# A long convolution per channel: four chunks joined by modal states in place of Toeplitz cross products

## What is computed

```
K = 2.0 * jnp.einsum('hn,hnl->hl', Cs, jnp.exp(P)).real    # P = dtA * l, 64 modes n per channel h, 1024 steps l
y = jnp.fft.irfft(u_f * k_f, n=n)[..., :Lq]                # causal convolution of each row with its channel's K
y = y + u_m * D[:, None]
x = x + y * mask                                           # the mask cuts each batch at its length
x = x + lora_8(x, adapter of the batch)                    # rank 16, 8 adapters
x = x + lora_64(x, adapter of the batch)                   # rank 16, 64 adapters
x = x + W[subject].T @ x + bias[subject]                   # 64x64 per batch
```

## Time and profile before

| | us |
|---|---|
| median of 3 runs (lowest, highest) | 754.1 (753.35, 757.32) |
| the profiled execution's own time | 756.05 |
| its span, first to last instruction | 754.2 |
| PE, DVE, ACT, POOL busy | 715.3, 576.9, 434.5, 380.6 |
| setup stage, in the span | 0 to 35.9 |
| turn 0 | 35.9 to 92.6 |
| turns 1 to 4 | 92.6 to 315.5 |
| turns 5, 6, 7 | from 315.5, 368.3 and 419.5; the last product ends at 468.5 |
| pair stage, from its first transposes | 479.0 to 754.2 |

### The profile page before, as it was taken

How to read it: one execution, slowest core, us unless ns; L and a number is a source line. 1 busy time by engine, 2 the same in 40 slices (tenths; PEclk the granted TensorE clock), 3 DMA queues, 4 the chain that set the end, 5 groups by cost and what they waited for, 6 DMA issues and landing times. The chain is left out here.

```text
span 754.2 us, 19782 instructions
## 1 busy us (share of the span) xinstructions
PE 715.3 (95%) x6685; PEld 538.6 (71%) x6685; DVE 576.9 (76%) x1116; ACT 434.5 (58%) x760; POOL 380.6 (50%) x680
## 2 busy tenths in 40 slices
PE   2699999999999999999899999699999999999997
PEld 2377687787787787777677777477767777776774
DVE  7687987887886776876667665288888888888885
ACT  4535645645635636636335332277777777777775
POOL 1000088888885000047777200667676676767663
PEclk9799999999999999999999999899999999999999
DMA  6488989999899899899888982789999999999973
GB/s 209 119 277 246 325 281 335 282 362 332 293 368 359 273 356 337 292 311 296 288 249 269 321 291 118 297 272 315 315 311 323 315 324 316 319 320 319 317 259 154
DMA packets 121719, 219.97 MB, mean 292 GB/s; under 512 B 20226, under 2 KB 80194, under 8 KB 121666
## 3 DMA queue, kind: packets, MB, share of 16 engines
q1 hardware_dynamic: 102546, 166.56, 68.2%
q10 hardware_dynamic: 9904, 33.59, 11.6%
q0 software_dynamic: 9216, 19.15, 7.9%
HBM read 146.35 MB, written 72.91 MB: 291 GB/s over the span
## 5 line engine op out<-in xcount | busy, mean ns | idle before, releaser
L1078 PE MATMUL ps<-toep,xTh 128*128 128x512 f16 (+3 forms) x1024 | 210.3, 301 | 4.3 <-DMA diff<-d_rows 3.4
L1078 PE MATMUL ps<-toep,xTl 128*128 128x512 f16 (+3 forms) x512 | 147.4, 301 | 0.0
L1078 PEld LDWEIGHTS ps<-toep,xTh 128*128 128x128 f16 x1024 | 97.5, 98 | 56.5 <-DMA diff<-d_rows 4.3
L825 POOL DMA_INDIRECT gnow<-g_rows,idx_g x64 | 59.6, 931 | 115.9 <-DMA g_rows<-g_out 89.6
L801 POOL DMA_INDIRECT wnow<-in_L_cond_weights,idx_w x64 | 62.6, 978 | 100.7 <-DVEq L1015 83.6
L1271 POOL DMA_INDIRECT asel<-a_rows,idx_a x64 | 72.0, 1125 | 77.5 <-PE ps L1417 76.4
L1044 DVE TENSOR_TENSOR ps<-ps,common 128x512 f32<-128x512 f32 x64 | 44.6, 697 | 66.3 <-ACT common L867 66.0
L1266 POOL COPY bsel<-bt 128x256 f16 x256 | 92.7, 405 | 2.8 <-issue 2.2
L1356 DVE TENSOR_TENSOR xTl<-ps,xTh 128x1024 f16<-128x1024 f32 x64 | 78.4, 1224 | 13.6 <-ACT xTh L1315 10.3
L1078 PE MATMUL ps<-diff,xTh 128*128 128x256 f16 x512 | 87.3, 273 | 0.0
L217 DVE TENSOR_TENSOR xTl<-ps,xTh 128x1024 f16<-128x1024 f32 x64 | 77.7, 1214 | 0.0
(11 more groups left out here) (231 smaller groups left out, 1719.2 us busy)
## 6 DMA issues: line engine op xcount, KB each, us to landing
toep<-k_rows SPq DMA_DIRECT2D x64, 384.0 KB, 6.1
diff<-d_rows SPq DMA_DIRECT2D x64, 384.0 KB, 7.3
xt<-in_x SPq DMA_DIRECT2D x32, 512.0 KB, 6.4
x_rows<-xt ACTq DMA_DIRECT2D x32, 512.0 KB, 4.9
xt<-x_rows SPq DMA_DIRECT2D x32, 512.0 KB
out_dram<-outt SPq DMA_DIRECT2D x32, 512.0 KB, 7.9
out_dram<-diff SPq DMA_DIRECT2D x32, 512.0 KB
toep<-x_rows SPq DMA_DIRECT2D x24, 512.0 KB, 7.4
```

The costliest lines, as they stand in the source:

```text
L825: gp.indirect_dma_start(m.gnow[:, v, :], None, m.g_rows, bass.IndirectOffsetOnAxis(ap=m.idx_g[0:64, q:q + 1], axis=0)).then_inc(g_gathered ...
L1078: last = PE.matmul(out, xs[x_part], rhs(part), start=start and k == 0, stop=stop and k == 2)
```

## The change

The convolution of a channel is cut into four chunks of 256 samples. Within a chunk it stays a Toeplitz product (`within`, with a matrix of 256 columns only). What earlier chunks do to a later one goes through the 128 modal states: `state` forms the state at the end of a chunk from its two blocks of x (table U, `ut`) and, for the second and third, from the state before (table R, `rt`, two numbers per mode spread over a matrix); `from_state` adds the state's effect to the next chunk (table V, `vt`). Each state leaves PE, is split by ACT (`high_state`) and DVE (`low_state`), and goes back to PE. One bank of PSUM holds the high half of the output, where there were two. The fourth chunk's last product (`finish_high`) runs behind the next channel's transposes.

The tables U, V and R are made per 8 channels by ACT, DVE and POOL, and POOL's own run of 32 units is cut up between its table work. The Toeplitz tables shrink from 768 to 128 KB a channel.

The diff, cut to its core:

```diff
+def high_state(nc, m, act, h, u, n):
+
+    act.wait_ge(m.s_done, 3 * h + n + 1)
+    nc.scalar.activation(m.sh[:, u % 2, n, :], state_bank(m, u, n), ACT.Copy, scale=1 / S_SCALE).then_inc(m.s_high, 1)
...
+def low_state(nc, m, dve, h, u, n):
+
+    dve.wait_ge(m.s_high, 3 * h + n + 1)
+    nc.vector.scalar_tensor_tensor(m.sl[:, u % 2, n, :], state_bank(m, u, n), 1 / S_SCALE, m.sh[:, u % 2, n, :],
+                                   ALU.mult, ALU.subtract).then_inc(m.s_ready, 1)
...
+def wide_products(nc, m, gp, k, e):
+
...
+    for n, part in enumerate((m.uc, m.us)):
+        nc.gpsimd.tensor_tensor(m.pu[:, :, :, n, :], part[:, :, cut, :], m.ue[:, :, cut, :], ALU.mult).then_inc(m.pu_ready, 1)
...
+def v_second(nc, m, gp, k, e):
...
+    nc.gpsimd.tensor_tensor(m.v2[:].rearrange("p q (a b) -> p q a b", b=TB),
+                            *by_steps(m, m.a2[:, KP * e:KP * e + KP, :], m.es, e), ALU.mult).then_inc(m.v2_ready, 1)
...
+def v_join(nc, m, dve, k, e):
+
+    dve.wait_ge(m.v1_ready, 2 * k + e + 1)
+    dve.wait_ge(m.v2_ready, 2 * k + e + 1)
+    nc.vector.tensor_tensor(m.v1[:], m.v1[:], m.v2[:], ALU.subtract).then_inc(m.v_made, 1)
...
+def turn_matrices(nc, m, gp, k, e):
+
...
+    for n, part in enumerate((m.rch, m.rcl)):
+        nc.gpsimd.tensor_tensor(m.rt[:, cut, n, :].rearrange("p q (s n) -> p q s n", s=2),
+                                m.eyeh[:].unsqueeze(1).unsqueeze(1).broadcast_to([P, KP, 2, N]),
+                                part[:, cut, :].unsqueeze(3).broadcast_to([P, KP, 2, N]), ALU.mult).then_inc(m.r_ready, 1)
...
-                def all_pairs(gather, keep, read):
-                    for q in range(U):
-                        gather(q)
-                    for k in range(PAIR_TURNS):
-                        if k < PAIR_TURNS - 1:
...
-                            for q in range(U * (k + 1), U * (k + 2)):
-                                gather(q)
-                        keep(k)
...
+                for i in range(TURNS):
+                    if i:
+                        turn_matrices(nc, m, gp, i, 1)
+                    else:
+                        turn_matrices(nc, m, gp, 0, 1)
+                    v_second(nc, m, gp, i, 1)
+                    if i == 1:
...
+                    if 1 <= i <= 5:
+                        w_unit(3 * i - 3)
+                    if i < TURNS - 1:
+                        wide_products(nc, m, gp, i + 1, 0)
+                        turn_columns(nc, m, gp, i + 1)
+                        turn_matrices(nc, m, gp, i + 1, 0)
+                        if 1 <= i <= 5:
+                            w_unit(3 * i - 2)
+                        if i == 6:
+                            for k in range(0, 5):
+                                g_unit(k)
+                        v_second(nc, m, gp, i + 1, 0)
+                        wide_products(nc, m, gp, i + 1, 1)
+                        if 1 <= i <= 5:
+                            w_unit(3 * i - 1)
+                        if i == 5:
+                            w_unit(15)
+
+                            gp.wait_ge(m.g_stored, 16 * G)
+                            for q in range(U):
+                                gather_g(q)
+                for k in range(5, PAIR_TURNS):
+                    g_unit(k)
...
+                        high_state(nc, m, act, h, u, 0)
+                        if not (last and u == XU - 1):
...
+                        high_state(nc, m, act, h, u, 1)
...
+                        if u == 2:
+                            if first:
...
+                        if make_k and u == 3:
+                            narrow_pairs(nc, m, act, i + 1)
+                            wide_cos(nc, m, act, i + 1)
...
+                        high_state(nc, m, act, h, u, 2)
...
+                        if make_k and u == 0:
+                            narrow_exp(nc, m, act, i + 1)
+                            wide_exp(nc, m, act, i + 1)
+                        if make_k and u == 1:
+                            narrow_trig(nc, m, act, i + 1)
+                        if make_k and u == 2:
+                            wide_sin(nc, m, act, i + 1)
+                            wide_abs(nc, m, i + 1)
+                        if make_k and u == 4:
+                            high_u(nc, m, act, i + 1, 0)
+                        if start_k and u == 6:
+                            act.wait_ge(m.pu_ready, 4 * i + 8)
+                            load_modes(m, act, i + 2)
+                        if make_k and u == 7:
+                            high_u(nc, m, act, i + 1, 1)
...
+                        if group and u % U == 1:
+
+                            act.wait_ge(a_loaded, 16 * g)
+                            S.activation(by_k.rearrange("p (k a r) -> p k a r", k=J, a=8),
+                                         nat_a.rearrange("p (a k r) -> p k a r", a=8, k=J), ACT.Copy).then_inc(a_ordered, 1)
...
+                        low_state(nc, m, dve, h, u, 0)
+                        if u == 0:
+                            low_u(nc, m, dve, i, 1)
+                        if u == 1:
+                            v_join(nc, m, dve, i, 1)
+                        if make_k and u == 3:
+                            narrow_mix(nc, m, dve, i + 1)
+                        if make_k and u == 4:
+                            k_first(nc, m, dve, i + 1, 3)
+                        if make_k and u == 5:
+                            low_u(nc, m, dve, i + 1, 0)
+                        if start_k and u == 7:
+                            narrow_turns(nc, m, dve, i + 2)
+                        if not (first and u == 0):
+
+                            dve.wait_ge(conv_done, h)
+                            select(h - 1, u - 1, 1, x1_ready)
+                        low_state(nc, m, dve, h, u, 1)
                         if not (last and u == XU - 1):
                             low_x(nc, m, dve, h + 1, u + 1)
...
+                        select(h, u, 0, low_ready)
+                        low_state(nc, m, dve, h, u, 2)
+                        if u == 0:
+                            v_first(nc, m, dve, i, 1)
                         if make_k and u == 1:
-                            k_tables(nc, m, dve, i + 1)
-                        if make_k and u == 3:
-                            k_first(nc, m, dve, i + 1, 3)
+                            wide_fraction(nc, m, dve, i + 1)
+                        if make_k and u == 2:
+                            narrow_modes(nc, m, dve, i + 1)
+                        if u == 2:
+                            low_v(nc, m, dve, i, 1)
                         if make_k and u == 4:
+                            v_first(nc, m, dve, i + 1, 0)
                             k_low(nc, m, dve, i + 1, 3)
...
+                        if make_k and u == 5:
+                            v_join(nc, m, dve, i + 1, 0)
+                        if make_k and u == 6:
+                            low_v(nc, m, dve, i + 1, 0)
+                        if group and u % U == 1:
...
+                    out = state_bank(m, u, n)
+                    if n == 0:
+                        pe.wait_ge(m.xTl_ready, h + 1)
+                        if v % KP == 0:
+                            pe.wait_ge(m.u_ready, 2 * i + 1 + u // KP)
+                    for b in range(2):
+                        for k, (x_part, part) in enumerate(((m.xTh, 0), (m.xTl, 0), (m.xTh, 1))):
+                            last = PE.matmul(out, m.ut[:, b, v, part, :], x_part[:, u % 2, 2 * n + b, :],
+                                             start=(b == 0 and k == 0), stop=(n == 0 and b == 1 and k == 2))
+                    if n:
+                        pe.wait_ge(m.s_ready, 3 * h + n)
+                        if n == 1 and v % KP == 0:
+                            pe.wait_ge(m.r_ready, 2 * (2 * i + v // KP + 1))
+                        for k, (part, before) in enumerate(((0, m.sh), (0, m.sl), (1, m.sh))):
+                            last = PE.matmul(out, m.rt[:, v, part, :], before[:, u % 2, n - 1, :], start=False, stop=(k == 2))
+                    last.then_inc(m.s_done, 1)
...
+                def from_state(i, u, c):
...
+                    pe.wait_ge(m.s_ready, 3 * h + c)
+                    if c == 1 and u % KP == 0:
+                        pe.wait_ge(m.v_ready, 2 * i + u // KP + 1)
...
                         if not (last and u == XU - 1):
                             turn(i, u + 1)
-                        convolve(i, u, first and u < 2)
-                        g = 2 * i - 1 + u // U
+                        if not (first and u == 0):
+                            if u:
+                                finish_high(i, u - 1)
...
+                        pe.wait_ge(m.toep_loaded[u % U], 16 * (2 * i + 1 + u // U))
+                        if not (first and u == 0):
+
+                            pe.wait_ge(low_ready, h)
+                        within(u, 0)
+                        state(i, u, 1)
+                        within(u, 1)
```

(10 more changed lines are left out.)

671 lines of the change are left out of this document (375 added, 296 removed).

## The result

The changed kernel took **886.2 us** (median of 4, 885.7 to 887.8) beside 755.7 us for the kernel before on the same chip: ratio 1.173, 95% interval 1.167 to 1.178. Slower was forecast, and the place of the largest single stall; but 886 is 60 us above the forecast and 30 above the end of its range.

A forecast was written before the change was run, and what follows sets the result against it. PE was taken as the bound, spending columns. Setup +5, turns 1 to 4 +29, turn 6 +27 and the tail +11, together +72 on 756.05, gave 828 us, 826 for the median; 8-in-10 range 775 to 856.

The forecast's parts named there:

- Turn 6 and POOL's 64 us: PE stands 24.5 us in turn 6 behind five adapter units (+27 for the turn); POOL works 64 us in turn 7.
- Rival (d): DVE's join of V does not wait for POOL's gathers, if POOL had passed them early enough; no chance of its own.
- A plain channel of PE: A channel's products and transposes take PE 5.22 us, against 6.10 before; -56 us over 64 channels if nothing waits.
- rival (b): Local waits vanish wholly and PE stays the bound: 748 us; chance 0.13.
- Turns 1 to 4: Four group turns at 48.1 us of PE, 14 of waits and 1 more: 252 against 222.9, +29 us.
- The walk through the queues: PE's waits for ACT, DVE and POOL, read from their queues: about 5 us a plain turn, below 14 a group turn.
- rival (c): DVE and POOL block each other at SBUF: 5 us a turn passed on, POOL delayed 2, +25: 852 us; chance 0.17.
- four in ten: Of some 19 added DVE operations a turn, four in ten meet POOL and lose 0.6 us: 5 us a turn.
- Turn 5 and turn 0: Turn 5 takes 53 us against 52.8 and turn 0 57 against 56.7: 0 for both.
- Setup: The first tables' longer chain of steps on ACT, DVE and POOL lengthens setup by 5 us, bounds 3 to 8.
- The tail: Turn 7 to the pair stage: POOL 64 us, barrier 2, filler matmuls 4.5, so 70.5 against 59.5: +11.
- rival (a): POOL's waits come, local ones mostly don't: 2 us a plain and 6 a group turn; 784 us; chance 0.24.

The follow-up runs named there:

- e2: The changed kernel without the channel stage's gathers and the W and adapter units, their tables zeroed at the head of POOL's program: 820.5 us.
- e6: The changed kernel with POOL's W and adapter units at other places of its program, all work kept: 831.7 us.
- e5: The changed kernel with idle products on PE in its two known waits of each group turn, ahead of the transposes of a: 873.1 us.
- e3: e2 with one channel of four in POOL's products for U, V and R from turn 2's tables on, later results wrong: 793.0 us.
- e1: The changed kernel with V's second product ahead of the five adapter units on POOL, in turn 6 alone: 883.9 us.
- e8: e6 with ACT's copy of a earlier and DVE's low part of U's second half at the end of channel 1: 819.9 us.
- e14: e6 with ACT's copy of a earlier, POOL's first adapter gathers behind V's second product, and DVE's low part of b ahead of table work: 794.2 us.
- e11: e14 plus idle products in PE's waits, DVE's table work behind the copy PE waits for, and 36 memsets behind POOL's last unit: 827.6 us.
- e12: e11 with the 36 memsets ahead of POOL's last three adapter units: 835.6 us.
- e15: The kernel before with 120 memsets on POOL behind its last adapter unit: 11 us to leave the stage, no total given.
- e16: e2 with 66 memsets on POOL behind its last product: 0.5 us to leave the stage, no total given.

## Why the prediction was right and wrong

**Turn 6 and POOL's 64 us: right.** The stall was 25.2 us for 24.5, through the instructions named, and POOL's work of turn 7 took 64.7 for 64. That the whole of turn 6 came out at 79.0 for 78.5 is in part luck: at a clock of 0.83 PE was busy for 47.0 us, not 41.8, and waited 32.0, not 36.7. e2 and e6 show that both go with the units. Rival (d) had no ground; e6 confirms that the place of the units is what matters.

**A plain channel of PE: right.** Channels 2 to 5 of turn 7 are 5.18 to 5.19 us for 5.22. So rival (b) would have been right about the work; it fell because the waits are there, in full.

**Turns 1 to 4: the step that failed, 34 of the 58 us.** The working had 48.1 us of PE, 14 of waits and 1 for the port, 252 for four turns; measured 285.6.
- Waits: 285.6 - 222.7 = 62.9 us, 15.7 a turn, against 15. The walk through the queues gave the right total. It had the parts less well: 3.4 us at `turn_a` of channel 1 as forecast and 1.2 behind `k_low` for 1.4, but 6.7 instead of 2.4 at channel 5, where V's join comes late because of the W unit, and less elsewhere.
- The same work at a lower clock: 18.5 us (e5). **No term of the sum had it.** The working priced PE at the full clock while it put 15 us of waits into each turn; all rows it priced from stood in stretches where the clock was 0.97 or 1.00. Waits of 2 to 7 us, several a turn, are what it falls after.
- PE's own work at full clock: 204.2 us for 192.4, 3 a turn. The 24 products of a join take 16.29/8 = 2.0 us on average, not 1.4: 2.2 or more in the six of turns 1 to 3, at a granted clock of 1.00 too, and 1.5 in the two of turn 4, as in all eight before (12.0/8). Turns 1 to 3 run as a loop and turn 4 is written out, but so they were before; why is open. The products for K (0.4) were left out. The rest of some 1.3 us a turn is not assigned.

**The port, rival (c): right in kind, wrong in its count.** In turns 1 to 4 some ten DVE instructions were lengthened, by about 12 us in all: 3 a turn, where "four in ten" gave 5. They are fewer and each costs more than the 0.6 us assumed: DVE's low part of U took 2.8 to 3.0 us at channel 0 of most turns, V's join 1.75 on average for 1.2. POOL's own instructions in these turns were lengthened by some 15 us. e3 puts the whole price, with the clock it takes along, at 27 us (20 in the profiled execution); the term had 1.5 a turn. Nor does the trace of before show the price "only once": some 16 DVE instructions of its turns 1 to 4 are lengthened, by about 12 us in all, while PE stood for 1.4 us there in all. The row was misread too: DVE ended at 105.07, 0.28 us behind POOL (104.79), not "just as POOL's did", about as if its 0.42 us had begun when POOL was done.

**Turn 5 and turn 0.** Turn 5 missed by 7.8: PE is busy for 46.6 us instead of 41.8 at a clock of 0.94, and waits 14 instead of 11. Turn 0 was 1.1 off. Against the true borders of before, though, these two turns lost 11.0 and 4.3 us where the forecast had none: its bases of 52.8 and 56.7 were each about 3.2 us too high, and those of turns 1 to 4 and of turn 6 as much too low.

**Setup: +9.9 for +5, beyond its bound of 8.** The chain was walked with free durations, but in the setup POOL and DVE work on the same tables at the same time: V's second product took 2.99 us for 1.96, U's 2.25 for 1.27, the second for R 2.02 for 1.04, both low parts 2.1 for 1.2. Together that is 4.7 us more than the durations priced. How much of it lies in the chain is not shown by any run.

**The tail: +20.2 for +11.** POOL's part was right; "2 for the barrier" was 11.0. The prediction names no row for it. In the kernel before, PE stood for 2.4 us there while POOL had been idle for 48.9, so that trace could show nothing of POOL's own leaving.

**What decided against rival (a)**, given 0.24: its argument was that ACT and DVE might run ahead of PE. They don't; the waits came to 15.7 us a turn. Its sum has a slip as well: by its own terms turn 0 gives -3, not -7, and the total 788, not 784.

## What to carry to other kernels

When a change turns a TensorE-bound stage into one that waits, price its matmuls a second time at the lower clock: here 63 us of waits took 18 us more with them. In strictly ordered queues, ask of every work unit what stands behind it on its own engine, including waits that guard a DMA (e1, e6), and do so again for the place it is moved to (e8): the order alone was worth 92 of the 130 us lost (e14). A barrier's price read where an engine came early says nothing of that engine coming last.

## What was not expected of the hardware

- Leaving the channel stage took GpSimd 10.9 to 11.0 us wherever it had issued gathers there and came last (the changed kernel, e11, e12, e15), and 0.5 us without gathers (e16).
- 200 idle matmuls made the kernel 13 us faster, where PE otherwise stood for 3.4 and 6.7 us; with waits of 1.4 us they made no difference.
- A two-input instruction of VectorE beside GpSimd's products took 2.8 to 3.0 us for 1.2, in most turns at the same place. The Trainium skill (page "SBUF — State Buffer", section "Who interferes with whom") has one of the two block the other for the whole instruction. The traces agree: the 2.77 us are 1.2 behind the V product of 1.96 us that had begun 0.27 us earlier, and the 3.41 us of V's join in turn 6 are 1.2 behind two U products of 1.26 and 1.25. GpSimd's first gather issued behind such a meeting took 1.8 us for 0.94.
